# Last expert's results on a plane of their own, and the tail's sums by TensorE in eight PSUM banks

## What is computed

```
xn = _layernorm(x, axis=-1)
s = _L1_attn_ref(xn, ...)
...
buf = zeros((E, capacity, H)).at[flat_e, slot].add(dispatched)
h = silu(einsum('ech,ehf->ecf', buf, w1))
out_buf = einsum('ecf,efh->ech', h, w2)
pair_out = out_buf[flat_e, slot] * keep[:, None]
combined = sum(pair_out.reshape(N, K, H) * k_probs[..., None], axis=1)
return combined.reshape(B, T, H) + x          # x is xn here
...
x = x + s * silu(that)
```

## Time and profile before

| | |
|---|---|
| median of 3 runs | 1201.26 us (1200.7 to 1201.7) |
| the profiled execution | 1198.16 us, of which the span is 1196.4 us |
| PE, DVE, ACT, POOL busy | 85%, 72%, 64%, 51% of the span |
| mean granted TensorE clock | 0.969 |
| end of the mixture stage | 985 to 1010 us: PE busy 3.9 of 25 us |
| expert stage, steady | 1010 to 1140 us: PE busy 121 of 130 us |
| last results land | 1166.4 us |
| end of the span | 1196.4 us |

### The profile page before, as it was taken

One profiled execution on the slowest core, in us unless ns is written; L12 is line 12 of the kernel. 1 busy time (PEld: TensorE's weight loads), 2 busy tenths in 40 slices (PEclk: granted clock), 3 DMA queues, 4 the chain that ended last, 5 costly groups with the idle time before them and its releaser, 6 DMA issues. The chain is left out here.

```text
span 1196.4 us, 18222 instructions
## 1 busy us (share of the span) xinstructions
PE 1020.0 (85%) x5064; PEld 420.9 (35%) x5064; DVE 864.0 (72%) x1769; ACT 766.1 (64%) x1460; POOL 612.6 (51%) x634
## 2 busy tenths in 40 slices
PE   4699999999998999779989998898998951999955
PEld 3123333333333322123444344344443421555532
DVE  4698989898989898846767776777666742566633
ACT  1066766667676777657776767676767730778741
POOL 5422323332332312347677777786869653366663
PEclk9999999999999999989999999999999975999988
DMA  2462824131321402688988789899999712622116
GB/s 62 76 134 66 198 77 103 38 58 41 53 64 29 75 11 59 184 220 205 222 176 207 168 200 166 202 172 195 180 192 176 158 46 97 231 82 82 56 36 211
DMA packets 118643, 149.74 MB, mean 125 GB/s; under 512 B 18219, under 2 KB 72091, under 8 KB 118108
## 3 DMA queue, kind: packets, MB, share of 16 engines
q1 hardware_dynamic: 111740, 139.65, 51.7%
q0 software_dynamic: 6272, 8.94, 2.4%
q10 hardware_dynamic: 544, 0.13, 0.2%
HBM read 109.44 MB, written 40.04 MB: 125 GB/s over the span
## 5 line engine op out<-in xcount | busy, mean ns | idle before, releaser
L738 ACT ACTIVATE a_probs<-a_score 128x512 f32<-128x512 f32 x512 | 293.1, 597 | 125.4 <-PE a_score L819 118.6
L916 DVE TENSOR_REDUCE a_mx<-a_mxps 128x2 f32<-128x1024 f32 x256 | 305.7, 1212 | 37.8 <-PE a_mxps L810 37.2
L1392 POOL TENSOR_TENSOR m_hidl<-m_hid,m_hidh 128x512 f16<-128x512 f32 x224 | 260.6, 1176 | 112.5 <-ACT m_hidh L1442 106.3
L1638 DVE TENSOR_TENSOR m_hid<-m_h,p_gates 128x512 f32<-128x512 f32 x216 | 147.0, 685 | 76.4 <-ACT m_h L1448 70.0
L1448 ACT ACTIVATE m_h<-m_h 128x512 f32<-128x512 f32 (+1 forms) x264 | 153.4, 582 | 42.7 <-PE m_h L1544 40.3
L1442 ACT ACTIVATE m_hidh<-m_hid 128x512 f16<-128x512 f32 x224 | 139.3, 622 | 49.1 <-DVE m_hid L1638 31.4
L831 PE MATMUL a_ops<-a_probs,a_vst 128*32 128x512 f32 x1024 | 136.4, 605 | 0.8 <-ACT a_probs L738 0.8
L1935 POOL DMA_INDIRECT t_picked<-e_yrow,e_rows x88 | 87.0, 989 | 74.4 <-DVE e_yrow L2069 51.4
L1522 PE MATMUL m_y<-m_hidh,p_wdh 128*128 128x512 f16 (+1 forms) x264 | 100.5, 381 | 19.9 <-POOL m_hidl L1392 17.9
L819 PE MATMUL a_score<-a_qstack,a_kstack 128*128 128x512 f16 x256 | 96.9, 384 | 8.6 <-ACT a_probs L738 7.0
L819 PE MATMUL a_score<-p_gates,p_raw 128*128 128x512 f16 x256 | 98.4, 384 | 5.9 <-ACT a_probs L738 4.3
(11 more groups left out here) (228 smaller groups left out, 1876.5 us busy)
## 6 DMA issues: line engine op xcount, KB each, us to landing
p_gates<-t_cw SPq DMA_DIRECT2D x256, 256.0 KB, 6.6
t_slots<-p_blank SPq DMA_DIRECT2D x8, 723.9 KB
e_rows<-t_slots SPq DMA_DIRECT2D x8, 723.9 KB
t_qparts<-a_qparts SPq DMA_DIRECT2D x32, 128.0 KB
t_picked<-p_blank SPq DMA_DIRECT2D x8, 512.0 KB
p_raw<-up SPq DMA_DIRECT2D x8, 512.0 KB, 5.4
p_raw<-down SPq DMA_DIRECT2D x8, 512.0 KB, 6.4
p_gates<-t_picked SPq DMA_DIRECT2D x16, 256.0 KB, 4.2
```

Source lines behind the costliest of these rows:

```text
L738: act.activation(probs[:, kt % 2, g, :], score[:, g % 2, :], ACT.Exp, scale=SCALE / (QS * QS)).then_inc(exp_done, 1)
L916: dve.tensor_reduce(mx[ahead % 2][:, j // 2, g:g + 2], mxps[:, j % 2, :, :], AX.X, ALU.max).then_inc(mx_done, 1)
L1392: pool.tensor_tensor(hidl[0:r0, k % r, :], hid[0:r0, k % r, :], hidh[0:r0, k % r, :], ALU.subtract).then_inc(lo_done[0], 1)
L1638: dve.tensor_tensor(gated, h, gates[:, q % (SLOTS * GROUP), :], ALU.mult).then_inc(mul_done, 1)
```

## The change

1. **The last expert's results** go to a DRAM plane `last` of their own, which takes the place of `xn1`: the mixture stage stores xn there, and for expert 7 DVE adds xn to the weighted result (four `scalar_tensor_tensor` for a block of four tiles in place of one `tensor_tensor`), and POOL scatters the sum over it. The last address column is therefore the bare token.
2. **Loads earlier.** The three first loads of places are issued at the end of the mixture block, as soon as the sends have landed; expert 0's in two parts, of which the first (4 of 11 tiles) suffices for the first block.
3. **The order in the expert stage.** `XLAG` 3 to 4, `XRING` 5 to 6; ACT's `result_out(B-1)` in f = 3; PE's and DVE's treatment of a result now for `B-2`, in f = 1 (f = 0 for the last expert's blocks).
4. **The tail.** SP loads all eight pieces of both planes of `picked` as soon as the seventh expert's results have landed, during the last expert, and after the last results only the 2 MB of `last`. DVE adds the two planes of each piece; PE puts that sum into eight banks (those of `e_h`, `e_x`, `e_o`, `e_y`) and adds `last` when it lands. Even pieces are finished by DVE; for odd pieces DVE makes 0.5 * s1 * g in one instruction and POOL adds x1. Results leave from four buffers of their own.

```diff
@@ Ahead, new functions
+    def place_buffers(self, nc, ctx):
+        self.rows_in = [ctx.enter_context(nc.sbuf_tensor(f"p_rows{k}", [CR, CT, REC], F32)) for k in range(XBUFS)]
...
+def load_places(sp, scratch, pre, e):
+    k = e % XBUFS
+    mine = scratch["slots"][PLACES * e:PLACES * e + PLACES, :].rearrange("(p t) c -> p t c", t=CT)
+    if e == 0:
+        head = slice(0, CT // 3 + 1)
+        sp.dma_start(pre.rows_in[k][:, head, :], mine[:, head, :]).then_inc(pre.first_in, 16)
+        mine, tiles = mine[:, head.stop:, :], slice(head.stop, CT)
+    else:
+        tiles = slice(0, CT)
+    sp.dma_start(pre.rows_in[k][:, tiles, :], mine).then_inc(pre.x_in[k], 16)
@@ mixture_phase, SP
+            for p in range(2):
+                sp.wait_ge(sent[p], 16 * SENDS * PASSES)
+            for e in range(XBUFS):
+                load_places(sp, scratch, pre, e)
             sp.wait_ge(x_out, 16 * BATCH)
             sp.wait_ge(xn_out, 16 * BATCH)
             sp.wait_ge(s_out, 16 * BATCH)
-            for p in range(2):
-                sp.wait_ge(sent[p], 16 * SENDS * PASSES)
@@ mixture_phase, DVE
+                        dve.tensor_scalar(rec[b.p][:, :, REC - 1:].bitcast(I32), mine, 1.0, None, ALU.mult).then_inc(placing, 1)
@@ expert_phase
-XLAG = 3
+XLAG = 4
-XRING = 5
+XRING = 6
@@ SP
+            for b in range(NB):
+                sp.wait_ge(put[b], put_by(b, E1 - 1))
+            both = scratch["picked"].rearrange("(k n p t) d -> n p k (t d)", k=K1, p=P, t=TILES)
+            for n in range(PIECES):
+                sp.dma_start(pick[n], both[n]).then_inc(pick_in[n // 2], 16)
             for b in range(NB):
                 sp.wait_ge(put[b], put_by(b, E1))
...
             for n in range(PIECES):
+                sp.dma_start(kept["last"][:, n, :], pieces(scratch["last"])[n]).then_inc(last_in[n], 16)
+            for n in range(PIECES):
+                sp.wait_ge(added[n % 2], n // 2 + 1)
+                sp.dma_start(pieces(io["out"])[n], done[n % OUTS][:]).then_inc(out[n % OUTS], 16)
@@ POOL
+                    plane = scratch["last"] if e == E1 - 1 else scratch["picked"]
...
+            for n in range(1, PIECES, 2):
+                pool.wait_ge(scaled_done, n + 1)
...
+                pool.tensor_tensor(done[n % OUTS][:], pick[n][:, 1, :], kept["x1"][:, n, :], ALU.add).then_inc(added[1], 1)
@@ ACT
-                if f == 2 and B:
+                if f == 3 and B:
                     result_out(B - 1)
@@ PE
-                if f == FC - 1 and B:
-                    result_turned(B - 1)
+                if f == int(B < ALL - NB) and B >= 2:
+                    result_turned(B - 2)
             for g in range(FC * ALL - XLAG, FC * ALL):
                 down(g)
+                if g == FC * ALL - XLAG:
+                    result_turned(ALL - 2)
             result_turned(ALL - 1)
             for n in range(PIECES):
                 pe.wait_ge(base_done, n + 1)
+                if n == XBANKS + 1:
+                    pe.wait_ge(row_done, ALL)
+                pe.matmul(piece_bank(n), ident[:], pick[n][:, 0, :], start=True, stop=False)
+            for n in range(PIECES):
+                pe.wait_ge(last_in[n], 16)
+                pe.matmul(piece_bank(n), ident[:], kept["last"][:, n, :], start=False, stop=True).then_inc(sum_full, 1)
@@ DVE
+                if e == E1 - 1:
+                    for t in range(nt):
+                        op = dve.scalar_tensor_tensor(yrow[b][:, t, :], ops[0:CR, P * t:P * t + P], rows[:, t0 + t, D + e:D + e + 1],
+                                                      rows[:, t0 + t, 0:D], ALU.mult, ALU.add)
...
+                if f == int(B < ALL - NB) and B >= 2:
+                    result_rows(B - 2)
+            result_rows(ALL - 2)
             result_rows(ALL - 1)
             for n in range(PIECES):
+                dve.wait_ge(pick_in[n // 2], 2 * 16)
+                dve.tensor_tensor(pick[n][:, 0, :], pick[n][:, 0, :], pick[n][:, 1, :], ALU.add).then_inc(base_done, 1)
+            for n in range(PIECES):
...
+                if n % 2:
+                    dve.scalar_tensor_tensor(pick[n][:, 1, :], bank, 0.5, kept["s1"][:, n, :], ALU.mult, ALU.mult
+                                             ).then_inc(scaled_done, 1)
+                    continue
+                dve.tensor_tensor(bank, bank, kept["s1"][:, n, :], ALU.mult).then_inc(scaled_done, 1)
...
+                dve.scalar_tensor_tensor(done[n % OUTS][:], bank, 0.5, kept["x1"][:, n, :], ALU.mult, ALU.add
+                                         ).then_inc(added[0], 1)
```

More of the change, by code:

```diff
@@ L43 @@
 NOWHERE = 1 << 20
+XBUFS = 3
 WS = 64.0
@@ L1849, in expert_phase @@
         wuh, wul, wdh, wdl = pre.wuh[1], pre.wul[1], pre.wdh[1], pre.wdl[1]
-        rows_in = [sb(f"rows{k}", [CR, CT, REC]) for k in range(XBUFS)]
+        rows_in, x_in = pre.rows_in, pre.x_in
         xh, xl = ([sb(f"{n}{k}", [P, 512], F16) for k in range(2)] for n in ("xh", "xl"))
@@ L1854, in expert_phase @@
         yrow = [sb(f"yrow{k}", [CR, n, D]) for k, (_, n) in enumerate(BLOCKS)]
[L1855 to L1858, removed]
+        kept = {n: sb(n, [P, PIECES, TILES * D]) for n in ("x1", "s1", "last")}
+        held = [t.rearrange("p (k b x) -> p k b x", k=K1, x=TILES * D) for t in (
+            pre.gates[:].rearrange("p s t -> p (s t)"), pre.raw[:].rearrange("p a n x -> p (a n x)"))]
+        pick = [held[n // 4][:, :, n % 4, :] for n in range(PIECES)]
+        done = [sb(f"done{j}", [P, TILES * D]) for j in range(OUTS)]
         hps, yps = ps("h", [P, XBANKS, 512]), ps("y", [P, 2, 512])
         xps, ops = ps("x", [P, 512]), ps("o", [P, 512])
-        x_in = [sem(f"x_in{k}") for k in range(XBUFS)]
         xT_full, xh_done, xl_done = sem("xT_full"), sem("xh_done"), sem("xl_done")
@@ L1868, in expert_phase, with piece_bank @@
         kept_in = sem("kept_in")
-        pick_in = [sem(f"pick_in{j}") for j in range(PBUFS)]
-        base_done, sum_full, g_done, scaled_done, added = (sem(n) for n in ("base", "sum", "g", "scaled", "added"))
-        out = [sem(f"out{j}") for j in range(PBUFS)]
+        pick_in, last_in = [sem(f"pick_in{n}") for n in range(PIECES // 2)], [sem(f"last_in{n}") for n in range(PIECES)]
+        base_done, sum_full, g_done, scaled_done = (sem(n) for n in ("base", "sum", "g", "scaled"))
+        added = (sem("dve_added"), sem("pool_added"))
+        out = [sem(f"out{j}") for j in range(OUTS)]
+        def piece_bank(n):
+            return hps[:, n, :] if n < XBANKS else (xps[:], ops[:], yps[:, 0, :], yps[:, 1, :])[n - XBANKS]
         def at(B):
@@ L1917, in _ @@
-            for n in range(PBUFS):
-                load_picks(n)
-            for n in range(PIECES):
-                sp.wait_ge(added, n + 1)
-                sp.dma_start(pieces(io["out"])[n], done[n % PBUFS]).then_inc(out[n % PBUFS], 16)
-                if n + PBUFS < PIECES:
-                    load_picks(n + PBUFS)
-            for j in range(PBUFS):
-                sp.wait_ge(out[j], 16 * (PIECES // PBUFS))
+            for n in range(PIECES):
+                sp.dma_start(kept["last"][:, n, :], pieces(scratch["last"])[n]).then_inc(last_in[n], 16)
@@ L1928, in _ @@
+            for n in range(PIECES):
+                sp.wait_ge(added[n % 2], n // 2 + 1)
+                sp.dma_start(pieces(io["out"])[n], done[n % OUTS][:]).then_inc(out[n % OUTS], 16)
+            for j in range(OUTS):
+                sp.wait_ge(out[j], 16 * (PIECES // OUTS))
         @block.gpsimd
@@ L1982, in _ @@
                 act.wait_ge(sum_full, n + 1)
-                bank = hps[:, n % XBANKS, :]
-                act.activation(bank, bank, ACT.Silu).then_inc(g_done, 1)
+                act.activation(piece_bank(n), piece_bank(n), ACT.Silu).then_inc(g_done, 1)
         @block.tensor
@@ L1990, in rows_turned @@
                 e, b, t0, nt = at(B)
-                pe.wait_ge(x_in[e % XBUFS], 16 * (e // XBUFS + 1))
+                if B == 0:
+                    pe.wait_ge(pre.first_in, 16)
+                else:
+                    pe.wait_ge(x_in[e % XBUFS], 16 * (e // XBUFS + 1))
                 if B:
```

89 lines of the change are left out of this document (32 added, 57 removed).

## The result

| | before | after |
|---|---|---|
| median of 6 runs each (range) | 1201.14 us (1200.50 to 1201.76) | 1205.44 us (1202.66 to 1207.33) |
| profiled execution, its span | 1198.16, 1196.4 us | 1204.4, 1202.4 us |

The ratio is 1.0038, 95% interval 1.0027 to 1.0050: the change makes the kernel 4.3 us slower. Forecast were 3.5 us less.

A forecast was written before the change was run, and what follows sets the result against it. Bounds were seen in the gap between stages, PE's expert stage with its `e_xl` and `e_yT` waits, and the end. Terms -4.5 + 7.8 + 1.5 - 8.3 gave -3.5 us: 1194.7 profiled, 1197.8 median; range 1187 to 1202.5.

The forecast's parts named there:

- The step that failed: Mixture stage, up to about 990 us: one more small DVE instruction per placing delays nothing; 0 us.
- The order: Expert stage: transposes ahead of `up` of f = 2 delay its silu and `e_xl`; 7.8 us lost.
- Rival A: Expert stage: the later transposes cost nothing or take waits away; 1190.0 us, down to 1187; chance 0.20.
- The sign for it: Expert stage: waits for `e_yT` gone, their time going into those for `e_xl`, from 9.2 to about 17 us.
- The last expert's first result to the landing: End of expert stage: four DVE instructions 1.1 instead of 0.68 us, scatters unchanged; stretch 0.4 us longer.
- Rival C: Last scatters: DVE's two-input SBUF sums hold up POOL's scatters, 5.5 us late, 1203.3 us; chance 0.12.
- The tail: Last scatter's landing to the end of the span: 21.7 us instead of 30.0, 8.3 less.
- rival D: Tail: PE at full level throughout (2.5 us), drain ending with the last store (1.8 us); 1193.5 us; chance 0.12.
- The bound of 7.3: Program's end: upper bound in us for POOL's drain behind its last addition; 5.3 was taken, lower bound 3.5.
- The head: Between mixture and expert stages: earlier loads let PE start at the block's release; gain 4.5 us, bounds 3.0 and 4.5.
- rival B: Expert stage: PE's granted clock falls below about 0.95 of full, costing 6.8 us, 1204.6 us; chance 0.06.
- the three places: Where the prediction said the change counts: between the stages, the expert stage, the end.

The follow-up runs named there:

- a1: Changed kernel, the last address column written by a scalar_tensor_tensor with one operand from PSUM instead of an SBUF-to-SBUF tensor_scalar: 1198.31 us, ratio 0.9974.
- b1: Kernel before, plus one 128x4 SBUF-to-SBUF tensor_scalar per batch into a tile nothing reads: 1206.95 us, ratio 1.0048.
- a3: Changed kernel with the expert stage's order put back to that of the kernel before: 1199.02 us, ratio 0.9978.
- b2: Kernel before with the expert stage's new order alone: 1208.43 us, ratio 1.0055.
- e1: Kernel of a4 with all eight final additions on DVE, none on POOL: 1207.34 us, ratio 0.9888, on a slower chip (before 1220.37).
- f3: Changed kernel, column from PSUM, results turned after the third up-projection, all final additions on DVE: 1189.06 us, ratio 0.9904 (before 1201.33).
- a4: Changed kernel with the edits of a1 and a3 together: 1208.76 us, ratio 0.9898, on a slower chip (before 1220.67).

## Why the prediction was wrong

- **The step that failed** is the sentence "Up to about 990 us the change alters nothing that waits: one more small DVE instruction in each placing, beside POOL's sends". The instruction waits itself, for POOL's subtraction, in seven batches: 7 x 0.8 = 5.6 us. Undone it gives 7.1 us back by runs (a1), added alone it costs 6.0 (b1). With this term, 6.0 to 7.1 us, the same sum gives 1203.8 to 1204.9, where 1205.4 was measured. The other 3 to 4 of the 10 us between the two profiled executions are not the change's: kernels without a held instruction show 386.4 to 389.8 us between SP's stores and end the mixture stage between 1008.6 and 1015.9 us, and before stood at the lower end (its profiled execution, 1198.16, was 3 us below its median). The trace of before had the price: line 187's 1340 ns beside the same POOL instruction, where it otherwise takes 682. It also had a hint that the prediction read only for scatters and the tail: two instructions with everything in SBUF that held each other up. It should have asked of each new DVE instruction where its operands lie, and what POOL does then.
- **The order** was right in kind and close in size: 7.65 against 8.9 us in its stretch; undone it gives 6.4 us by runs (a3), alone it costs 7.4 (b2). Rival A (1190.0) is refuted. The sign for it was off: the wait for `e_xl` was to grow to about 17 us and grew to 24.4, since the 9 us that left the wait for `e_yT` went there too, as the prediction's own sentence says but its number doesn't. That only the place ahead of `up` of f = 2 costs would be too narrow: one `up` later there are still 3.7 of the 7.7 us, with a result two blocks later and a lag of 4. What this rest hangs on no run takes apart.
- **The last expert's first result to the landing** was 1.1 us longer instead of 0.4. Its four instructions took 1.13 us from first to last (each 0.34, the upper bound, but they overlap), as forecast 1.1. The rest is in three scatters of 1.13, 1.45 and 1.09 us instead of 0.99, each of which met one of DVE's sums (others met one and kept 0.99): from the first one's start to the last one's 13.6 us instead of 12.9. Rival C, which had 5.5 us, is there in kind, at an eighth of the size.
- **The tail** came to the forecast 21.7 us by two errors. PE had the 2.4 GHz level (granted clock 1.00) from 1184 to 1192, so the sums were ready 2 us earlier, as in rival D; and POOL's drain ended 7.3 us behind its last addition, as in the kernel before, not 5.3. The bound of 7.3, from the same stage, was the better choice. That the two errors cancel is luck. e1 and f3 show that this drain sets the end: with no addition on POOL the span ends with SP, 3.6 to 4.2 us earlier.
- **The head** gained what was forecast, 4.5 us.
- **The clock** (rival B) has no part in it that a run shows: 0.96 before and 0.96 after over 130 us of the expert stage (1010 to 1140, and 1020 to 1150 with the later start).

The range reached to 1202.5 us; the chance of slower was 0.15. Neither held a mechanism outside the three places.

## What to carry to other kernels

A DVE `tensor_scalar`, or one with two inputs, that has all its operands in SBUF waited here for the rest of POOL's current instruction when POOL computed from SBUF, however small it was (128x4 elements: 0.8 us each time). Give it an operand in PSUM, or put it where POOL is idle, and look for such neighbours in the trace before costing a small instruction at nothing. An engine's drain can be the critical path of a block's end: POOL's ended 5.3 and 7.3 us behind its last work here, so POOL shouldn't work last. And where work is moved out of a wait, ask what the next instruction behind its new place releases: the wait for a copy went, and the one behind it grew by more.

## What the hardware showed that I had not expected

- 128x4 elements on DVE, from SBUF to SBUF, took 945 to 961 ns beside a POOL subtraction of 1.16 us and 151 to 163 ns beside none; with one operand in PSUM 149 to 156 ns, POOL busy or not. A `batch_norm_aggregate` from SBUF to SBUF kept its 148 to 183 ns beside POOL.
- POOL's drain was still open long after its last instruction: 12.4 us from its start at the mixture's end (5.3 behind the last scatter), 8.6 us at the end of the program (7.3 behind the last addition, and 7.3 behind the last scatter where POOL had no addition). SP's took 7 ns.
- On two of the chips used, ACT stood still in each expert with its input there, once or twice, for up to 2.6 us in a4 and 3.3 in others, and the expert stage took 18 to 20 us longer (153.7 and 156.2 against 135.9 us for the same kernel). Only on these did the later turning beat the old order, by 5 to 6 us. The cause is open.
